# A transformer block with two routed layers on one core: earlier second routing, slot numbers on GpSimd, scatters without filling writes

## The reference, cut to what matters

```python
def ffn(x, Wr, br, W1, b1, W2, b2):             # xf: 4096 rows of 128
    logits = xf @ Wr.T + br                     # 8 experts
    expert_idx = argmax(logits)                 # the first of equal ones
    h = relu(einsum('td,efd->etf', xf, W1) + b1)    # 512 wide
    y = einsum('etf,edf->etd', h, W2) + b2
    return y[expert_idx, arange(4096)]          # one expert for each row

x = x + 0.5 * ffn(layernorm(x), ...)
x = x + attention(layernorm(x), ...)            # 16 sequences of 256, 16 heads of 8, rms norm, rotary, softmax
x = x + 0.5 * ffn(layernorm(x), ...)
```

## Time and profile before

| | us |
|---|---|
| median of 3 runs (481.8 to 483.8) | 482.72 |
| the profiled execution, its own time | 479.99 |
| its span | 478.2 |
| busy in the span: PE 427.5, DVE 382.0, ACT 349.1, POOL 349.1 | |

### The profile page before, as it was taken

One profiled execution on the slowest core, in us unless ns is written; L12 is line 12 of the kernel. 1 busy time (PEld: TensorE's weight loads), 2 busy tenths in 40 slices (PEclk: granted clock), 3 DMA queues, 4 the chain that ended last, 5 costly groups with the idle time before them and its releaser, 6 DMA issues.

```text
span 478.2 us, 14075 instructions
## 1 busy us (share of the span) xinstructions
PE 427.5 (89%) x4140; PEld 318.0 (66%) x4140; DVE 382.0 (80%) x1055; ACT 349.1 (73%) x782; POOL 349.1 (73%) x561
## 2 busy tenths in 40 slices
PE   7999999989878898999989998998888979899993
PEld 4347999767764565665656665565455559789993
DVE  4786788897888788988889889988888557687772
ACT  4416776777747998989989898888677947467771
POOL 8019898978857988698683974399766807798995
PEclk9899999999999999999999999999999999899998
DMA  7872434251100000000000000000011123223310
GB/s 205 252 290 57 95 86 152 64 178 42 29 25 18 14 15 14 13 8 14 10 14 2 3 3 3 2 13 14 21 36 37 36 54 80 74 71 96 77 33 13
DMA packets 28651, 27.03 MB, mean 57 GB/s; under 512 B 5685, under 2 KB 25948, under 8 KB 28019
## 3 DMA queue, kind: packets, MB, share of 16 engines
q1 hardware_dynamic: 24034, 17.65, 12.4%
q0 software_dynamic: 4544, 8.49, 6.6%
HBM read 16.56 MB, written 12.71 MB: 61 GB/s over the span
## 4 chain that ended last, share of the span: by engine, by line
PE 41%; DVE 23%; issue 12%; POOL 12%; ACT 7%; DMA 2%; DVEq 1%; ACTq 0%; POOLq 0%
DVE Smax L1769 8%; PE PS L862 8%; PE PS L878 8%; PE PS L1005 5%; PE PS L958 5%; PE PS L981 4%; POOL out L632 3%; PE PS L940 3%; POOL Unread L603 2%; DVE St L1388 2%; DMA Pt<-rows,TokI 2%; ACT Pt L1231 2%; PE PS L924 2%; PE PS L917 1%; PE PS L1035 1%
## 5 line engine op out<-in xcount | busy, mean ns | idle before, releaser
L1769 DVE TENSOR_REDUCE Smax<-PS 128x4 f32<-128x1024 f32 x128 | 155.8, 1224 | 30.8 <-PE PS L958 30.0
L1231 ACT ACTIVATE Pt<-PS 128x1024 f32<-128x1024 f32 x128 | 126.4, 1024 | 18.4 <-PE PS L981 15.1
L878 PE MATMUL PS<-W,HsT 128*128 x624 | 85.2, 280 | 3.7 <-DVE Ys L1640 3.6
L862 PE MATMUL PS<-XsT,Ws 128*128 128x128 f32 x624 | 84.0, 278 | 1.0 <-ACT XsT L1135 0.7
L878 PEld LDWEIGHTS PS<-W,HsT 128*128 128x128 f32 x624 | 76.8, 194 | 6.7 <-issue 5.7
L862 PEld LDWEIGHTS PS<-XsT,Ws 128*128 128x128 f32 x624 | 77.3, 194 | 4.5 <-ACT XsT L1135 1.9
L1005 PE MATMUL PS<-Pt,Vg 128*32 128x256 f32 x1024 | 68.5, 385 | 0.4
L705 POOL TENSOR_TENSOR HL<-Rn,Zero 128x512 fp32r<-128x512 f32 x28 | 35.3, 1283 | 38.1 <-DVE Rn L1752 36.6
L610 POOL DMA_INDIRECT Pt<-rows,TokI x39 | 40.3, 1034 | 29.9 <-DVE TokI L1586 19.4
L603 POOL MEMSET Unread<- 128x352 f32 (+1 forms) x140 | 62.0, 443 | 0.2
L958 PE MATMUL PS<-QkT 24*128 24x256 f32 x512 | 59.7, 306 | 2.0 <-DVE Smax L1769 1.7
(11 more groups left out here) (255 smaller groups left out, 725.2 us busy)
## 6 DMA issues: line engine op xcount, KB each, us to landing
AtCol<-slots SPq DMA_DIRECT2D x39, 65.5 KB, 1.9
rows<-XX SPq DMA_DIRECT2D x8, 288.0 KB, 4.3
XX<-x SPq DMA_DIRECT2D x8, 256.0 KB, 4.2
W<-w1T SPq DMA_DIRECT2D x2, 1024.0 KB, 6.2
W<-w2T SPq DMA_DIRECT2D x2, 1024.0 KB, 9.1
mid<-mid_second SPq DMA_DIRECT2D x1, 1472.0 KB
mid<-Ys SPq DMA_DIRECT2D x16, 64.0 KB
QkT<-NmaxT SPq DMA_DIRECT2D x64, 4.0 KB
```

Of the source, the lines that this page charges most:

```text
L862: last = nc.tensor.matmul(PS[:, h_bank(n) + c // 2, (c % 2) * P:(c % 2 + 1) * P], Ws[:, n % R_WS, c * P:(c + 1) * P], XsT[:, n % 2, :], st ...
L878: last = nc.tensor.matmul(PS[:, y_bank(n), 0:P], HsT[:, n % 2, c, :], W2[:, ds(e * D_FF + c * P, P)], start=(c == 0), stop=(c == FC - 1))
L1231: nc.scalar.activation(Pt[:, m % 2, 2 * pair:2 * pair + 2, :, :].rearrange("p h c t -> p (h c t)"), PS[:, score_bank(m, pair):score_bank(m ...
L1769: nc.vector.tensor_reduce(Smax[:, b % 2, :, at:at + 33:32].rearrange("p t h -> p h t"), PS[:, max_bank(m, pair):max_bank(m, pair) + 2, :]. ...
```

## The change

It moves and replaces work at many places; the attention's mathematics and the matrix products stay.

- Start of `experts(1)`: `full_table` now makes the entries of tiles 0 to 12 (`FIRST_FULL` = 13) from lots 0 and 1 at step 58, and SP reads these tiles once lots 0 and 1 are stored. Tiles 13 to 18 get their entries from `more_tiles` (step 63) and `more_table` (tiles 1 to 5). PE does the first transposes and the first `up` inside step 64, ahead of the last `values`; DVE makes the first three weight copies (`weights`, step 61). Step 64 on ACT stands behind the first `relu`. The nine filling products and those of step 50 are gone.
- Routing: one scan for a whole lot in place of eight; the slot numbers (`lot_slots`) are made by POOL, six instructions for a lot, in place of DVE; layer norm and logits of lot 2 too; parts of lots 0 and 1 are spread over later steps; the last lot's first parts stand in tiles 6 and 7, so that Run is ready two tiles ahead of `rank`.
- Bias: in `experts(1)` ACT copies Bs (four buffers) beside Ws, in place of DVE. The load of the expert's number stands right behind `relu` on DVE.
- POOL's stream in `experts(1)`: layer norm and logits of the last lot ahead of scatter 0; the last lot's stores behind scatter 3, each with a write of 352 columns; no write behind scatters 4 to 38.
- Drains: at step 29, ahead of the last lot's layer norm, and ahead of the scatter of tile 27 (`DRAIN_TILE`).
- `rope_tables` in the first ffn sets up FreshLot by five memsets.

The diff, cut to its core:

```diff
-POOL_NORM_AT = {32: 0, 45: 1}
-POOL_LOGITS_AT = {35: 0, 48: 1}
...
+POOL_NORM_AT = {32: 0, 44: 1, 57: 2}
+POOL_LOGITS_AT = {35: 0, 46: 1, 58: 2}
...
+TABLE_AT, SCALE_AT, MORE_AT = 58, 62, 63
+FIRST_FULL = ROUTE_LOTS[1][1] - N_EXP + 1
...
-STORES_BEHIND = 8
+STORES_BEHIND = 3
+DRAIN_TILE = 27
...
-FILL_TURN, FILL_MAXIMA, FILL_END = {50: 5}, {58: 6}, 9
+FILL_MAXIMA = {58: 6}
...
-LAST = {"norm": 3, "inverse": 6, "logits": 4, "rank": 9}
+LAST = {"norm": 0, "inverse": 5, "rank": 9}
...
             sp.wait_ge(offs_ready, 1)
-            for i in range(LAST_LOT):
-                sp.wait_ge(lot_out[i], 16 * (ROUTE_LOTS[i][1] - ROUTE_LOTS[i][0]))
...
+            for i in range(2):
+                lot_stored(i)
+            for t in range(FIRST_FULL):
+                fetch_tile(t)
+            sp.wait_ge(offs_ready, 2)
+            lot_stored(2)
+            for t in range(FIRST_FULL, FULL):
                 fetch_tile(t)
...
             def scatter(t):
...
-                if t < S_TILES - 2:
+                if t <= STORES_BEHIND:
                     pause(LONG_PAUSE)
...
+            def over_experts(into, values, r, op):
+
+                lot_link(nc.gpsimd.tensor_tensor(Half[:, r], values[:, r, 0:4], values[:, r, 4:8], op))
+                lot_link(nc.gpsimd.tensor_tensor(Half[:, r, 0:2], Half[:, r, 0:2], Half[:, r, 2:4], op))
+                lot_link(nc.gpsimd.tensor_tensor(into[:, r], Half[:, r, 0], Half[:, r, 1], op))
+
+            def lot_slots(i):
+                r = LOT_ROWS[i]
+                shape = [P, r.stop - r.start, N_EXP]
+                pool.wait_ge(*emptied("rank", i))
+                lot_link(nc.gpsimd.tensor_tensor(Place[:, r], by_tile(SeenE, r), Base[:].unsqueeze(1).to_broadcast(shape), ALU.add))
+                lot_link(nc.gpsimd.tensor_tensor(Place[:, r], Place[:, r], by_tile(HotE, r), ALU.mult))
+                over_experts(SlotF, Place, r, ALU.add)
+                nc.gpsimd.tensor_copy(SlotI[:, r], SlotF[:, r]).then_inc(lot_ready, 1)
...
-            nc.gpsimd.drain()
             for t in range(S_TILES):
                 if t == LAST["norm"]:
+                    nc.gpsimd.drain()
                     lot_layernorm(N_LOT + 1 + LAST_LOT)
-                if t == LAST["logits"]:
                     lot_logits(LAST_LOT)
+                if t == DRAIN_TILE:
+                    nc.gpsimd.drain()
                 scatter(t)
                 if t == STORES_BEHIND:
+                    lot_slots(LAST_LOT)
                     for j in range(*ROUTE_LOTS[LAST_LOT]):
                         place(LAST_LOT, j)
...
+                if n == TAIL - 1:
+                    pe.wait_ge(exp_ready, 2 * n - 1)
+                    begin()
                 if n < 0 or not group(n + QKT_LEAD):
                     small(n)
+                if n == TAIL - 1:
+                    first()
                 if group(n - 1):
                     values(n - 1)
...
                     copy(Ws[:, n % R_WS, :], W1[:, ds(e * D_FF, D_FF)]).then_inc(ws_ready, 1)
+                    if k:
+                        if t >= R_BS:
+                            act.wait_ge(hA_ready, n - R_BS + 1)
+                            act.wait_ge(hB_ready, relus(n - R_BS + 1))
+                        copy(Bs[:, bias(n), :], B1T[:, ds(e * FC, FC)]).then_inc(bs_ready, 1)
...
             def seen(r):
-                for e in range(N_EXP):
-                    last = nc.vector.tensor_tensor_scan(Seen[:, r, e], OneCol[:, r], Hot[:, r, e], 0.0, ALU.mult, ALU.add)
-                return last
+                return nc.vector.tensor_tensor_scan(flat(SeenE, r), FreshLot[:, N_EXP * r.start:N_EXP * r.stop], flat(HotE, r), 0.0, ALU.mult, ALU.add)
```

More of the change, by code:

```diff
@@ L27 @@
 R_WS = 3
+R_BS = 4
 R_YS = 6
@@ L161, in program @@
         SeenE = sb("SeenE", [P, N_EXP, N_TILES], BF16)
-        Hot, Seen = (e_major[:].rearrange("p e j -> p j e") for e_major in (HotE, SeenE))
+        Half = sb("Half", [P, N_TILES, N_EXP // 2])
+        FreshLot = sb("FreshLot", [P, N_EXP * N_TILES], BF16)
         Mx = sb("Mx", [P, N_TILES])
@@ new lines, in begin, with first, run @@
+                def begin():
+                    pe.wait_ge(slots_ready, k + 1)
+                    x_transpose(0)
+                def first():
+                    up(0)
+                    x_transpose(1)
+                def run():
+                    for t in range(1 if k else 0, S_TILES + 1):
+                        if k and t - 1 in TABLES:
+                            pe.wait_ge(slots_ready, TABLES[t - 1])
+                        if t < S_TILES:
+                            up(t)
+                        if t >= 1:
+                            e = pe.value_load(tile_expert(k, t - 1), min_val=0, max_val=N_EXP - 1)
+                        if k and t == LAST["rank"]:
+                            rank(LAST_LOT)
+                        if not k and tail(t):
+                            max_scores(t - TAIL_TILE, 0)
+                        if k:
+                            for n in DRAIN.get(t, ()):
+                                step(n)
+                        if t + 1 < S_TILES:
+                            x_transpose(t + 1)
+                        if t >= 1:
+                            down(t - 1, e)
+                        if not k:
+                            if t == WP_TURN:
+                                wp_turn()
+                            if t == WP_ROUTER:
+                                wp_router()
+                            for n in RAMP_PE.get(t, ()):
+                                step(n)
@@ L915, in fill_const @@
+                return begin, first, run
             def fill_const(count, bank=7):
@@ L1124, in _ @@
             pe.wait_ge(b2_ready, 1)
-            experts(0)
+            begin, first, run = experts(0)
+            begin()
+            fill_const(FILL_FIRST[1])
+            run()
+            begin, first, run = experts(1)
             for n in range(RAMP_END, TAIL):
                 step(n)
-            fill_const(FILL_END, 3)
-            experts(1)
+            run()
         @block.scalar
@@ L1195, in run @@
                     for t in range(S_TILES):
-                        if k:
-                            for n in DRAIN_FIRST.get(t, ()):
-                                step(n)
-                        first = not tail(K0 + t) and not (k and t in DRAIN_SECOND)
+                        first = not tail(K0 + t) and not (k and t in DRAIN)
                         if first and t + 1 < S_TILES:
@@ L1367, in _ @@
             begin, run = experts(1)
-            for n in range(RAMP_END, TAIL):
+            for n in range(RAMP_END, TAIL - 1):
                 step(n)
-                if n == TAIL - 2:
-                    begin()
             run()
@@ L1423, in scaled_logits, with ranks, over_experts, settled @@
                 link(tt_(Lg[:, r], Lg[:, r], Br[:].unsqueeze(1).to_broadcast(shape), ALU.add))
+            def ranks(r):
+                return Rank[:].unsqueeze(1).to_broadcast([P, r.stop - r.start, N_EXP])
+            def over_experts(values, r):
+                return values[:, r].unsqueeze(2).to_broadcast([P, r.stop - r.start, N_EXP])
+            def settled():
+                dve.wait_ge(step_done, links[0])
+            def mark(ins):
+                links[0] += 1
+                ins.then_inc(step_done, 1)
@@ L1683, in reload @@
+                return weights, begin, run
             def reload(i):
@@ L1688, in rope_tables @@
                 half = HD // 2
+                link(nc.vector.memset(FreshLot[:], 1.0))
+                for r in LOT_ROWS:
+                    nc.vector.memset(FreshLot[:, N_EXP * r.start:N_EXP * r.stop:r.stop - r.start], 0.0)
                 dve.wait_ge(rope_in, 16 * 5)
@@ L1850, in step @@
                     full_table()
+                if n == WEIGHTS_AT:
+                    weights()
+                if n == SCALE_AT:
+                    begin()
+                if n == MORE_AT:
+                    more_tiles()
             def last_lot(t, place):
```

455 lines of the change are left out of this document (236 added, 219 removed).

## The result

The changed kernel takes 468.01 us (median of 4 runs, 467.83 to 468.64), the kernel before took 482.26 beside it (4 runs, 479.97 to 483.8): ratio 0.9718, 95% interval 0.9685 to 0.9751. The profiled execution took 467.86 us with a span of 466.1, against 479.99 and 478.2. So 12.1 us of span are gone.

| stage | before | after | gain | forecast |
|---|---|---|---|---|
| start to ACT's first exponential of attention | 144.4 | 143.5 | 0.9 | 0 |
| from there to the first exponential of the last group | 235.2 | 231.2 | 4.0 | 2.5 |
| from there to Xr of tile 0 | 7.5 | 3.8 | 3.8 | 4.8 |
| Xr of tile 0 to `up` of tile 4 | 10.1 | 12.4 | -2.3 | -1.6 |
| `up` 4 to `up` 18 | 32.6 | 26.7 | 5.9 | 5.0 |

What follows compares the result with a forecast made beforehand. TensorE binds the late tiles; what can be won lies before, between and behind that stretch. 4.8 + 3.1 + 4.1 + 2.5 = 14.5 us off 479.99 gives 465.5, plus 2.7: 468.2; 8 in 10: 463.5 to 475.

Steps and rivals of the forecast that it cites:

- Seam into the tiles: From attention to tile 0: tile 0 needs stores up to tile 19 only, so Xr starts 4.8 us earlier.
- In the tiles: Tiles of the second ffn: 4.3 us lost in place of 7.46, the wait for Run gone; gain 3.1 us.
- rival (d): PE falls to the lower clock in the seam, costing 1.7 us: 469.9; counted inside the forecast's 0.62.
- Tile 19: Second seam: Xr at 420.9 where steady progress wants 419.9, nearly absorbed, 0.3 us lost.
- End: Last output to span's end: scatters 1.28 us apart, GpSimd caught up, 3.1 us in place of 7.2; gain 4.1.
- Attention: Attention steps with lot work: slot numbers and scans leave DVE, gaining 2.5 of 4.2 us lost.
- Drains: GpSimd's four drains: 0.083 us for each indirect DMA since the one before, giving 5.9, 2.2, 2.7 and 1.0 us.
- The rule against it: GpSimd operations reading SBUF could hold up DVE's two-SBUF-input ones, 7 us at worst, total 7.5; left out of the sum.
- (c): Scatters 4 to 38 each wait for the one before to land, 2.2 us: slower, about 499; chance 0.05.
- (a): DVE stays the bound in tiles 0 to 16: tile term 0, seam 3.0, gain 9.6: 473.1; chance 0.14.
- (b): Attention gets nothing and the end half, as drains scale otherwise and GpSimd comes late: gain 8.4: 474.3; chance 0.12.
- The 2.7 between profile and median: Whole kernel: median 482.72 lay 2.7 us above the profiled 479.99; the same distance was added to 465.5.

Runs made afterwards that it cites:

- All moved: Changed kernel without writes behind the last lot's stores and scatters, nine fills on PE, scatters 0 to 5 first, third drain at tile 20: 465.17 us.
- the repeated one: The changed kernel measured again with no edit: 469.28 us, ratio 0.9732 to the kernel before.
- the last three versions: All moved (465.17 us), the same with scatters 0 to 3 first and rank in tile 8 (465.12), and with scatters 0 to 4 first (464.74).

## Why the prediction came out right, and where it did not

The forecast was 468.2, the median 468.01. The direction and the main mechanisms held: earlier stores bring the seam forward, the wait for Run and the fall of the clock behind it go, and scatters follow at 1.28. That the number came out within 0.2 is luck. Single terms were up to 1.5 us too small and up to 2.4 too large, their sum was 2.4 too large, and an offset that did not hold made up for it (last point below).

- **Seam into the tiles, 4.8:** 3.8 measured. The step itself held: the store of tile 19 sets Xr, 5.43 us behind its start where I used 5.95, PE then waits. But store 19 came 1.7 us ahead of the last group's exponential (373.11 and 374.77) where I had 3.3 (376.4 and 379.68). Ahead of lot 2's logits on GpSimd stood the stores of tiles 14 and 15 (363.99, 365.65), which I had not counted in its queue, so the first of the four began at 368.23.
- **In the tiles, 3.1:** 1.7 measured (-2.3 + 5.9 - 1.9). The wait for Run and the fall at tile 9 are gone, `up` 4 to 18 runs at 1.906, so I left 0.9 too much there. The front lost 2.3 instead of 1.6. PE fell to the lower clock there, rival (d), but DVE hides most of its price: the six profiles without a fall lost 1.2 to 2.2 there, so the 1.6 was sound and a fall adds some 0.5.
- **Tile 19, 0.3:** 1.9 measured, a step that failed outright. The chain that brings its rows came 1.1 us earlier than forecast (Xr 419.84 for 420.9), but steady progress 2.3 earlier (417.6 for 419.9). The difference lies on GpSimd: Base was there at 402.6, the slot numbers began at 403.09 behind scatter 3's write, took 1.9 instead of 1.7, and 0.81 of idle that I had not counted followed them. Xr came 6.1 us behind the last store's start and 4.5 behind scatter 4's: the two landed within 0.2 us of each other (417.55 and 417.75), so both bound the tile. "All moved" took scatter 4 away and kept the store, and the stall stayed; with the last store 1.3 earlier as well it went.
- **End, 4.1:** 1.7 measured. I expected the last scatter at 463.1, and it started at 463.19, by two errors that cancel: scatter 4 started 1.2 earlier than forecast, and the third drain took 3.6 instead of 2.7, with 0.81 of idle behind it that I had not counted. What failed is the output beside it, 460.56 instead of 462.7: in this execution GpSimd, not PE, sets the end, and the output's lead is worth nothing. In the repeated one, with PE 3.5 us later at `up` 38, the outputs set it, so the two are close. The terms of my sum were thus not independent: what attention and the tiles gave above the forecast, the end took back. The writes put back show how firmly GpSimd holds the end. Also "0.4 behind its output" was a misreading of the earlier trace rows: the scatter at 455.41 is that of tile 27, whose output was written at 451.24; the two rows belong to different tiles. A GpSimd that has caught up starts 1.09 behind an output's start, and the last scatter is 1.25 behind, in seven profiles with a caught-up GpSimd (1.20 in an eighth).
- **Attention, 2.5 of 4.2:** 4.0 measured. The pool of loss was undersized: against the changed kernel, steps 39 to 44 of the kernel before took 2.5 more and steps 51, 52 and 54 2.4, together 5.0 where I had doubled 1.35 + 0.64. New losses in steps 34, 47, 48 and 56 are 1.1. The drain is the 0.28 of step 34, which I had at nothing. The fills of step 50 are 1.0 of the 5.0, but step 62 gives them back.
- **Drains, 5.9 / 2.2 / 2.7 / 1.0:** 5.9, 2.2, 3.6 and 1.7. The law of 0.083 us for a DMA held for 97 (8.02), 71 and 45 (3.74 twice more), but for fewer it is only the lower level: 26 took 2.21 in six traces and 2.35 to 3.51 in five (and 2.35 to 2.37 as the third drain of the last three versions), 33 took 2.75 in four and 3.30 to 3.58 in four, the changed kernel's own among these. The four with 2.75 are the four in which PE had fallen to half clock behind tile 19, the other four are those in which it had not; what links the two I did not find. For 19 and 12 it took 1.96 and 1.67, above the law. The closing drain ends 2.65 behind the last scatter's start with 12 DMAs, close to the 2.2 after which SP saw its transfer, but 2.93 with 19, so a floor set by the landing alone does not explain it.
- **ACT's copy of Bs:** 0.19 a tile inside the idle time, pace 1.896, as forecast.
- **The rule against it,** the Trainium skill, SBUF — State Buffer, "SBUF: two separate sides": the traces agree that the two hold each other up, in small amounts and on either side. The same GpSimd operation (L691) in lot 2 and in the last lot, where DVE's Xr and its addition, both with two SBUF inputs, run beside it; then that addition beside GpSimd's slot numbers, all in the changed kernel:

```profile
362.13 0.21 POOL L691 TENSOR_TENSOR Dm<-Dm 128x6 f32<-128x6 f32 x1
393.08 0.54 POOL L691 TENSOR_TENSOR Dm<-Dm 128x6 f32<-128x6 f32 x1
393.26 0.28 DVE L1745 TENSOR_TENSOR AtCol<-AtCol,B 128x128 f32<-128x128 f32 x1
...
402.78 0.39 DVE L1745 TENSOR_TENSOR AtCol<-AtCol,B 128x128 f32<-128x128 f32 x1
...
404.47 0.29 POOL L768 TENSOR_TENSOR SlotF<-Half 128x6 f32<-128x6 f32 x1
404.70 0.28 DVE L1745 TENSOR_TENSOR AtCol<-AtCol,B 128x128 f32<-128x128 f32 x1
404.83 0.20 POOL L777 CAST SlotI<-SlotF 128x6 int32<-128x6 f32 x1
```

  In the twelve traces of the changed kernel and its versions the L691 operation takes 0.54 in all eleven places where these two run beside it and 0.20 to 0.21 in the thirteen others. The slot operation of L768 takes 0.28 to 0.31 in six traces beside the same pair and 0.20 in the other six. The addition takes 0.28 as a rule, also where GpSimd is idle, but 0.39 to 0.40 in nine traces beside the first slot operation and 0.58 in one; beside an indirect DMA or a write it is now and then 0.31 to 0.40. So each such meeting costs 0.1 to 0.3 us. No run tests what all of them cost together. The earlier trace rows already had it: an XN takes 0.34 us in most steps and took 0.37 and 0.47 in that pair, so "shows no such hold" was a misreading.
- **Rivals:** (c) is refuted, the distance is 1.28 to 1.40 from scatter 4 to 38 but for the drain. (a) is refuted by the 5.9 in tiles 4 to 18. (b) is half true: attention gave 4.0 where it had nothing, but the end gave 1.7, near its 1.0.
- **The 2.7 between profile and median** was not kept. The profiled run of after lies 0.15 under its median, so on the scale of profiles the forecast was 465.5 and the measurement 467.9: the sum was 2.4 too large, and the offset hid it. The profiled execution of the kernel before was one of its faster ones: beside the repeated run, its executions with a granted clock of 0.99 or more took 479.0 to 480.2 us, those with 0.979 took 482.9 to 484.5. So some 2 us of the 14.3 between the medians is clock that the kernel before loses in most executions and did not lose in its profile.

Open: the 0.9 us ahead of attention. That stage lies between 142.7 and 144.4 in all profiles of both kernels, so it need not come from the change.

## What to carry to other kernels

Ask of every engine with a backlog when it will have caught up, before you add the gains of the others: here removing the writes alone gave 1.8 us, the rest alone 1.2, and both together 13 to 14. When a transfer waits for several things, date all of them, up to its landing; a version that moves only one of two finds the other. Pair rows by tile before reading a lag or a wait from them. Before you say that two engines do not disturb each other, compare each one's operation with the same operation alone, on both engines.
